# Causal attention on one core: score banks seeded with minus the row maximum by ScalarE, maxima turned in 32x32 blocks and spread by DMA

## The reference

```python
latent_kv = x @ w_kv_down                # 256 -> 128
kv = latent_kv @ w_kv_up                 # keys and values of 16 heads of 64
q = x @ w_q
att = einsum('bqhd,bkhd->bhqk', q, k) * 64 ** -0.5
att = where(causal, att, -inf)
att = softmax(att, axis=-1)              # exp(att - max of the row) / sum
y = einsum('bhqk,bkhd->bqhd', att, v)
return y @ w_out
```

## Time and profile before

| | before |
|---|---|
| median of the runs | 2116.74 us |
| lowest and highest | 2111.61, 2118.76 us |
| span of the profiled execution | 2113.7 us |
| TensorE busy | 94% |
| VectorE busy | 63% |
| ScalarE busy | 52% |
| GpSimd busy | 67% |
| attention's exponentials, first and last start | 292.2 and 2014.6 us |

### The profile page before, as it was taken

How to read it: one execution, slowest core, us unless ns; L and a number is a source line. 1 busy time by engine, 2 the same in 40 slices (tenths; PEclk the granted TensorE clock), 3 DMA queues, 4 the chain that set the end, 5 groups by cost and what they waited for, 6 DMA issues and landing times.

```text
span 2113.7 us, 35206 instructions
## 1 busy us (share of the span) xinstructions
PE 1984.7 (94%) x12886; PEld 1240.9 (59%) x12886; DVE 1337.2 (63%) x2728; ACT 1097.9 (52%) x2236; POOL 1425.9 (67%) x812
## 2 busy tenths in 40 slices
PE   8997788999999999999989999999999999999898
PEld 6775454555655555555555655555555555555466
DVE  7786555576656666666665657576756575656443
ACT  5775543455545454545455444545445445444585
POOL 1333225778687878787857687868786878687822
PEclk9998899999999999999999999999999999999999
DMA  3000000000000000000000000000000000000001
GB/s 124 1 1 1 0 7 13 13 19 10 13 18 16 13 19 12 19 10 19 13 12 17 12 20 11 17 12 20 11 18 11 20 11 18 11 14 11 26 26 60
DMA packets 29243, 37.01 MB, mean 18 GB/s; under 512 B 6928, under 2 KB 20368, under 8 KB 29072
## 3 DMA queue, kind: packets, MB, share of 16 engines
q1 hardware_dynamic: 29072, 34.76, 5.4%
HBM read 30.02 MB, written 4.46 MB: 16 GB/s over the span
## 4 chain that ended last, share of the span: by engine, by line
PE 63%; DVE 14%; POOL 12%; ACT 6%; issue 4%; DMA 1%; POOLq 0%; ACTq 0%; SPq 0%; DVEq 0%
PE heads_out L918 16%; POOL acc L1416 10%; PE beside L723 9%; PE scores L723 7%; PE two_heads L874 7%; PE scores L897 4%; PE scores L903 4%; PE scores L899 4%; PE scores L901 4%; DVE part_max L1112 3%; ACT prob L1331 2%; PE two_heads L723 2%; PE beside L929 2%; PE heads_out L723 1%; DVE wQK_lo L1073 1%
## 5 line engine op out<-in xcount | busy, mean ns | idle before, releaser
L1416 POOL TENSOR_TENSOR acc<-acc,prob 128x1024 f32<-128x1024 f32 (+3 forms) x512 | 1017.9, 1988 | 195.4 <-ACT prob L1331 140.1
L1331 ACT ACTIVATE prob<-scores 128x512 f32<-128x512 f32 (+3 forms) x1280 | 579.4, 539 | 649.2 <-PE scores L903 289.0
L1112 DVE TENSOR_REDUCE part_max<-two_heads 128x2 f32<-128x1024 f32 x384 | 469.3, 1222 | 280.5 <-PE two_heads L874 279.7
L918 PE MATMUL heads_out<-prob,V 128*64 128x512 f32 (+3 forms) x2560 | 544.4, 547 | 0.0
L1109 DVE CUSTOM_DVE_ANT_0 two_heads<-two_heads,mask 128x128 f32<-128x128 f32 (+3 forms) x512 | 242.0, 514 | 180.4 <-PE two_heads L874 180.4
L874 PE MATMUL two_heads<-k_hi,q_hi 64*128 64x512 f32 (+3 forms) x1280 | 274.1, 424 | 62.8 <-DVE part_max L1112 30.6
L918 PEld LDWEIGHTS heads_out<-prob,V 128*64 128x64 f32 x2560 | 156.7, 137 | 232.4 <-issue 209.6
L874 PEld LDWEIGHTS two_heads<-k_hi,q_hi 64*128 64x128 f32 x1280 | 120.6, 184 | 256.6 <-issue 133.4
L897 PE MATMUL scores<-q_hi,k_hi 64*128 64x512 f32 (+3 forms) x1280 | 236.1, 364 | 0.8 <-DVE k_lo L1100 0.5
L903 PE MATMUL scores<-neg_max,sel 64*128 64x512 f32 (+3 forms) x1280 | 235.6, 362 | 0.0
L901 PE MATMUL scores<-q_lo,k_hi 64*128 64x512 f32 (+3 forms) x1280 | 235.5, 362 | 0.0
(11 more groups left out here) (301 smaller groups left out, 2898.7 us busy)
## 6 DMA issues: line engine op xcount, KB each, us to landing
rden<-rden_rows SPq DMA_DIRECT2D x128, 128.0 KB, 2.9
X<-u SPq DMA_DIRECT2D x8, 512.0 KB, 8.7
out<-X SPq DMA_DIRECT2D x8, 512.0 KB, 2.9
wQK_raw<-wQuery SPq DMA_DIRECT2D x16, 192.0 KB, 3.1
wO_raw<-wOut SPq DMA_DIRECT2D x16, 128.0 KB, 2.8
wV_raw<-wValue SPq DMA_DIRECT2D x8, 128.0 KB, 2.9
den<-den_rows SPq DMA_DIRECT2D x64, 4.0 KB
rden_rows<-den SPq DMA_DIRECT2D x64, 4.0 KB, 1.3
```

The lines of the kernel that those rows point to most:

```text
L918: made = pe.matmul(heads_out[head(h), x0:], V[vn % NVS][:, tt, p % 2, head(h)], prob[step % NPROB][:, h, x0:], start=t == 0, stop=t == TPB ...
L1112: made = ve.reduce_max(part_max[:, t, :, c:c + 1], two_heads[:, :, 0:width], AX.X)
L1331: ac.activation(prob[step % NPROB][:, h, x0:], bank(task, h)[:, x0:], ACT.Exp).then_inc(empty(task, h)[0], 1)
L1416: po.tensor_tensor(total[:, :, x0:], total[:, :, x0:], new[:, :, x0:], ALU.add).then_inc(acc_ok, 1)
```

## The change

The fourth pair of score matmuls goes, and `sel`, `neg_max` and the task `turn_max` with it.

- A task `seed` for each step stands an iteration ahead of its score: ScalarE writes minus the maxima, from SBUF into the columns of both score banks that the step uses, in one instruction over both heads. It waits until the banks are emptied. The score's three pairs of matmuls then add to what is there (none of them starts anew), once `seeded` has the seed's number. Where a bank of the step was last used by a task that doesn't write the whole of it, TensorE first runs an opening matmul on each bank (`opened`), and the seed waits for that.
- The maxima are needed on all 128 partitions, `top`, two slots (`NMAX` is 2). VectorE's `minus_max` reduces into the 8 first columns of a tile of 32 columns and transposes it in 32x32 blocks; `rows_out`, four DMAs, writes the rows to DRAM (`top_rows`, four slots); three iterations later `spread_max` reads 4 KB back onto each of the 128 partitions. The spread waits for the last seed of two units before.
- ScalarE takes the exponential of both heads in one instruction, which releases both banks; the score signals once for both. The mask in PSUM stays on VectorE.
- The counting of GpSimd's sums is split over two semaphores; `part_max` has its heads ahead of its tiles; `den` and some tiles lie elsewhere in SBUF; a value or project task starts its bank once, not once for each half.

```diff
@@ planner
+        elif kind == "seed":
+            _, idx, t = task
+            n = 2 * (self.step_of[idx, t] % 2)
+            self.seed_free[idx, t] = sorted({self.freed[b] for b in (n, n + 1) if self.freed[b]})
+            if not (self.whole[n] and self.whole[n + 1]):
+                self.opened[idx, t] = len(self.opened) + 1
+            self.seeds[idx, t] = len(self.seeds) + 1, list(self.count)
...
             idx = self.next_maximum()
             if idx is not None:
-                fillers.append((s + 2, self.start[idx] - 4, ("turn_max", idx)))
+                spreads.append((s + 2, "rows_out", idx))
...
             while self.at < goal - 1:
                 maximum()
+            if self.layers_done:
+                for step in steps[s + 2:s + 4]:
+                    self.need("seed", *step)
+            for at, kind, idx in spreads[:]:
+                if at <= s and (kind == "rows_out" or self.unseeded(idx - NMAX)):
+                    spreads.remove((at, kind, idx))
+                    self.need(kind, idx)
+                    if kind == "rows_out":
+                        spreads.append((s + 6, "spread_max", idx))
             for idx, t in steps[max(0, s - 2):s]:
                 self.need("weigh", idx, t)
@@ tensor_program
-                elif kind == "turn_max":
...
-                    for t in range(TPB):
-                        made = pe.transpose(bank(task)[:, t * P:(t + 1) * P], row_max[:, t, :, :].rearrange("p a b -> p (a b)"), ident[:, :])
-                    made.then_inc(full(task)[0], 1)
+                elif kind == "seed" and task[1:] in plan.opened:
...
+                    first = 2 * (step_of[idx, t] % 2)
+                    for h in range(2):
+                        made = pe.matmul(scores[:, first + h, :], axT_hi[:, 0, 0:P], axT_hi[:, 0, 0:BLK], start=True, stop=True)
+                    made.then_inc(opened, 1)
                 elif kind == "score":
...
-                    for h in range(2):
-                        pe.matmul(bank(task, h)[:, x0:], sel[head(h), :], neg_max[idx % NMAX][head(h), x0:], start=False, stop=True).then_inc(full(task, h)[0], 1)
+                    w.wait_ge(seeded, plan.seeds[idx, t][0])
...
+                    for n, (k, q) in enumerate(terms((k_hi[g], k_lo[g]), (q_hi[i], q_lo[i]))):
+                        for h in range(2):
+                            made = pe.matmul(scores[:, first + h, x0:], k[head(h), kc], q[head(h), x0:], start=False, stop=n == 2, skip_group_check=True)
+                    made.then_inc(full(task)[0], 1)
@@ vector_program
-                    ve.reduce_max(row_max[:, :, :, 0:1], part_max[:, :, :, 0:j + 1], AX.X).then_inc(row_max_ok, 1)
+                    ve.reduce_max(row_max[:, 0:2 * TPB].rearrange("p (h t) -> p h t", h=2), part_max[:, :, :, 0:j + 1], AX.X).then_inc(row_max_ok, 1)
+                    w.wait_ge(row_max_ok, idx + 1)
+                    ve.transpose(rows[:, idx % 2, :], row_max[:, :]).then_inc(rows_ok, 1)
@@ scalar_program
-                    ac.activation(neg_max[idx % NMAX][:, :], bank(task), ACT.Copy, scale=-1.0).then_inc(empty(task)[0], 1)
+                elif kind == "seed":
+                    _, idx, t = task
+                    x0 = P * max(0, t - TPB * UNITS[idx][2])
+                    first = 2 * (step_of[idx, t] % 2)
+                    w.wait_ge(*top_here(idx))
+                    if task[1:] in plan.opened:
+                        w.wait_ge(opened, plan.opened[idx, t])
+                    else:
+                        for b, n in plan.seed_free[idx, t]:
+                            w.wait_ge(emptied[b], n)
+                    ac.activation(scores[:, first:first + 2, x0:], top[idx % NMAX][:, :, x0:], ACT.Copy, scale=-1.0).then_inc(seeded, 1)
...
-                    for h in range(2):
-                        w.wait_ge(*full(task, h))
-                        ac.activation(prob[step % NPROB][:, h, x0:], bank(task, h)[:, x0:], ACT.Exp).then_inc(empty(task, h)[0], 1)
+                    ac.activation(prob[step % NPROB][:, :, x0:], scores[:, first:first + 2, x0:], ACT.Exp).then_inc(empty(task)[0], 1)
@@ sync_program
+                elif kind == "rows_out":
+                    idx = task[1]
+                    w.wait_ge(rows_ok, idx + 1)
+                    if idx >= NTOP:
+                        w.wait_ge(*top_here(idx - NTOP))
+                    for n in range(0, P, SQ):
+                        sp.dma_start(top_rows[idx % NTOP, :].rearrange("(a x) -> a x", x=P)[:, n:n + SQ],
+                                     rows[n:n + 2 * TPB, idx % 2, :]).then_inc(top_out[idx % 2], 16)
+                elif kind == "spread_max":
+                    idx = task[1]
+                    w.wait_ge(top_out[idx % 2], 64 * (idx // 2 + 1))
+                    if idx >= NMAX:
+                        w.wait_ge(seeded, plan.seeds[last_step(idx - NMAX)][0])
+                    sp.dma_start(top[idx % NMAX].rearrange("p h x -> p (h x)"), top_rows[idx % NTOP:idx % NTOP + 1, :].broadcast_to([P, 2 * BLK])).then_inc(top_in[idx % 2], 16)
```

More of the change, by code:

```diff
@@ L41 @@
          (8, "updated"): ["maximum"], (8, "mixed"): ["maximum", ("key", 1), ("query", 1), "maximum"],
-         (8, "tail"): [("turn_max", 0), ("latent", 0, 2), ("value", 0, 0)], (8, "products"): ["maximum", ("value", 0, 1)], (8, "end"): ["maximum"],
+         (8, "tail"): [("rows_out", 0), ("latent", 0, 2), ("value", 0, 0)], (8, "products"): ["maximum", ("spread_max", 0), ("value", 0, 1)], (8, "end"): ["maximum"],
          (9, "updated"): ["maximum"], (9, "mixed"): ["maximum", ("turn_tiles", 0, 12), "maximum"],
          (9, "products"): ["maximum"], (9, "end"): ["maximum", ("turn_tiles", 0, 14), "pair"], (10, "updated"): ["maximum", "pair"]}
+WHOLE = ("query", "key", "latent", "value", "project", "score")
 WAITING = {("ssm_front", 0): 48, ("turn", "a", 0): 14}
@@ L82, in __init__ @@
         self.side_bank = 7
-        self.kinds, self.nth, self.masked = {}, {}, {}
+        self.kinds, self.nth = {}, {}
+        self.whole, self.seeds, self.seed_free, self.opened, self.masked = [False] * 8, {}, {}, {}, {}
         self.start, self.step_of, self.at = [], {}, 0
@@ L95, in take @@
         for g in groups:
+            for b in g:
+                self.whole[b] = task[0] in WHOLE
             free = [self.freed[b] for b in g if self.freed[b]]
@@ L138, in add @@
             self.roots[task] = self.n_roots
-        elif kind in ("query", "key", "value", "turn_max", "latent", "denominators", "turn_tiles", "project"):
+        elif kind in ("query", "key", "value", "latent", "denominators", "turn_tiles", "project"):
             self.take(task, self.one_bank())
@@ L453, in early @@
         def early(task):
-            return self.layers_done or task[0] in ("turn_tiles", "latent") or task[1] < {"key": 2, "query": 2, "turn_max": 2, "value": 1}.get(task[0], 0)
+            return self.layers_done or task[0] in ("turn_tiles", "latent") or task[1] < {"key": 2, "query": 2, "value": 1}.get(task[0], 0)
         for s in range(0, len(steps) + 2, 2):
@@ L712, in attention_memory @@
         def attention_memory(w):
-            for kind in ("query", "key", "turn_max"):
+            for kind in ("query", "key"):
                 w.wait_ge(*full((kind, NU - 1)))
@@ L722, in product @@
                 for n, (l, r) in enumerate(pairs):
-                    made = pe.matmul(dst, l, r, start=first and n == 0, stop=last and n == len(pairs) - 1)
+                    made = pe.matmul(dst, l, r, start=first and n == 0, stop=last and n == len(pairs) - 1, skip_group_check=not first)
                 return made
@@ L939, in tensor_program @@
                         cs = slice((2 * half + q) * P, (2 * half + q + 1) * P)
-                        made = product(bank(task)[:, q * C:(q + 1) * C], terms((oT_hi[:, cs], oT_lo[:, cs]), (wO_hi[n % 2][:, :], wO_lo[n % 2][:, :])))
+                        made = product(bank(task)[:, q * C:(q + 1) * C], terms((oT_hi[:, cs], oT_lo[:, cs]), (wO_hi[n % 2][:, :], wO_lo[n % 2][:, :])), first=q == 0)
                     made.then_inc(full(task)[0], 1)
@@ L1117, in vector_program @@
                     if x0 >= 0:
-                        first = plan.bank[task][0][0][0]
+                        first = 2 * (step_of[idx, t] % 2)
                         w.wait_ge(att_const, 2)
-                        for h in range(2):
-                            w.wait_ge(*full(task, h))
+                        w.wait_ge(*full(task))
                         ve.tensor_tensor(scores[:, first:first + 2, x0:x0 + P], scores[:, first:first + 2, x0:x0 + P],
@@ L1320, in scalar_program @@
                     x0 = P * max(0, t - TPB * UNITS[idx][2])
+                    first = 2 * (step % 2)
                     if not step:
@@ L1404, in gpsimd_program @@
                     total, new = acc[idx % 2], prob[step % NPROB]
-                    for h in range(2):
-                        w.wait_ge(*empty(("score", idx, t), h))
```

(1 more changed line is left out.)

136 lines of the change are left out of this document (67 added, 69 removed).

## The result

| | before | after |
|---|---|---|
| median of the runs | 2115.32 us | 2308.86 us |
| lowest and highest | 2111.61, 2118.76 us | 2303.09, 2313.0 us |
| ratio, 95% interval | | 1.091 (1.0884 to 1.0936) |
| span of the profiled execution | 2113.7 us | 2301.8 us |
| mean granted clock | 0.980 | 0.947 |

The account below looks back on a forecast made before the run. TensorE, busy 94% of the span, was taken as the bound, with GpSimd second. The terms summed to 2113.7 - 115 + 30 + 20 + 5 = 2053.7 us of span; the forecast was 2050 us, range 1970 to 2120.

Parts of the forecast that it names:

- TensorE's relief: Score matmuls and transposes of maxima removed from TensorE: 160 us if always the bound, 115 us taken by the chain's share.
- a term for it: VectorE's second maximum of an iteration comes sooner after the first: 0.06 us for each of 320 iterations, 20 us added.
- The seeds' busy time is hidden.: ScalarE: about 83 us a group with seeds, below TensorE's 96 to 99, so the seeds' busy time costs nothing.
- The wait for bank 0: Seeds wait for VectorE to take a filler's rest from score bank 0: 50 x 0.6 = 30 us, bounds 0 and 100.
- Maxima run up to 20 steps ahead: DMA and SyncE: maxima complete some 20 steps ahead, so the spread costs nothing; 48 us if late.
- The clock: Rival (d), attention: granted clock 0.98, not the expected 1.00, costs 34 us, about 2090; 4 in 100.
- GpSimd as the next bound: GpSimd's 37.5 us meets TensorE's about 37 in the 41.8 us unit; nothing added beyond the chain's share.
- rival (b): GpSimd's sums and loss at unit changes hold the pace, 1 to 2 us a group won: 2085 to 2100; 16 in 100.
- (c): Rival: seeds too late every iteration, behind filler copies in ScalarE's queue; slower from 0.50 us wait, 2180; 14 in 100.
- signs of being wrong: Seeds over 1.1 us, score waits over 0.5 us in most iterations, attention clock under 0.98, or spread after first seed due.
- just in time: Replay of one full iteration: seeds end at 4.9 and 5.9 us, TensorE's next scores stand at 4.8 to 6.1.
- Rival (e): TensorE not relieved because banks must be opened at each step, or gains and waits cancel: 2110 to 2123; 6 in 100.

Follow-up runs that it names:

- b4: The kernel before without the fourth pair of score matmuls, nothing in its place, exponential's input scaled by zero: 2056.3 us, ratio 0.9734.
- e10: The changed kernel with the spread one iteration after the rows, seeds of 64 columns a head and the exponential's input scaled by zero: 2075.2 us.
- b1: The kernel before with an iteration's second filler in the side bank, not in score bank 0: 2261.6 us, ratio 1.0701.
- e6: The changed kernel with the spread one iteration after the rows, not three, and the second filler in the side bank, not score bank 0: 2255.8 us.
- e1: The changed kernel with the spread of the maxima one iteration after the rows are written, not three: 2211.5 us, ratio 1.0458.

## Why the prediction was wrong, point by point

- **TensorE's relief, 115 us with the pair's 89 to 125 in it.** Wrong: the pair is worth 57 us (b4). The turned maxima, 35 us of the 160, were never taken out by themselves. The step that failed is "line 903 stands in the whole chain with 89 us": a chain is followed back along the last releaser, and work that ended shortly before it isn't on it. In b4 it is the reduction of the maxima that moves up: the weight loads' wait for it goes from 72.3 to 137.5 us. How closely behind it had ended before was not measured. I had a term for it, 20 us with bounds 0 and 50; it belongs to the pair's removal, and by b4 it is at most 68.
- **The seed's duration, 1.03 us.** Right: 1026 ns.
- **"The seeds' busy time is hidden."** The worst step. I compared ScalarE's 83 us a group with TensorE's 96 and called the difference cover. In e10 a cut of 397 us of seeds gave 136 us, so 0.34 of each microsecond was paid where I had put none. "Without that cover each 0.1 us of seed would cost 64 us" was the sentence to keep: 0.62 us less a seed gave 136 us, that is 22 us for each 0.1. Busy sums hide nothing if the work stands in a ring of two bank pairs. Whether the 136 us come from the time that the banks are taken or from the place in ScalarE's queue stays open.
- **The wait for bank 0, 50 x 0.6 = 30 us, bounds 0 and 100.** Of the right kind and too small. I priced a seed behind a filler; the square b1, e6 shows the other side of it, that bank 0 was worth 147 us and is worth 44 in e1, 47 in the changed kernel. Seeds waited 105.0 us for project sums alone, which I had mentioned with "some project tiles like them" and not counted. The project filler's tie to GpSimd's `oT_lo` was in the code and in no term.
- **"Maxima run up to 20 steps ahead", spread at nothing, 48 us if late.** Wrong in its premise. The lead of 20 steps is that of a single maximum over the score step of the same number. A unit's last maximum is only about 22 less its own length ahead of its first score: 10 steps for a unit of 12. The rows go out 2 steps later, the spread 6 after that, and the seeds stand 2 ahead of the score: nothing is left. I checked the slots of the unit after a four-step one, and not this count. But the count alone doesn't make the stop: the 16-step unit's spread stands in the list just ahead of its first seeds too, and no seed of a 16-step unit waited for `top`, since SyncE went from its rows straight to its spread. The 12-step unit has both, no lead and two units' denominators' DMAs between its rows and its spread. I had named this queue ("SyncE also carries the `den` round trip") and priced it at 48 us if late; it cost 97 us, 16 stops of 5.5 us and what follows each.
- **The clock, 4 in 100 at 0.98.** It came to 0.93 to 0.98 in the stretches of 100 us from 400 to 2100. The waits were not spread but came as stops of some 5 us, with 0.60 in the six microseconds after one; in e1, without them, the mean of the whole kernel is 0.967, 0.947 with them.
- **GpSimd as the next bound.** Its chain share doubled, as rival (b) had it, and its busy share fell, from 67% to 62%. Shares of a chain that goes round in a circle name a member of the circle. Removing 778 us of its work gave 59 us.
- **The rivals.** (c), with 14 in 100, had the sign and a part of the place: seeds late in ScalarE's queue, decisive from 0.50 us an iteration, 2180. The seeds were of 1.03 us, not 1.28, and still it was 2309; TensorE's matmuls waited for seeds 130 / 320 = 0.4 us an iteration and its weight loads 217 / 320 = 0.7 us, which may partly be the same time; to this came GpSimd's 182 us more for `oT_hi`. Half of the loss, the 97 us of the late spread, was in no rival. It was among the signs of being wrong, as a spread that lands after its first seed is due, and so was a granted clock under 0.98 in attention; both came. What misled me was the replay of one iteration that fits "just in time": seeds that end at 4.9 and 5.9 us for scores that stand at 4.8 to 5.4 and 5.5 to 6.1 leave no room for any delay. Rival (e)'s first half can be ruled out: banks were opened in four steps, not in each.

## What to carry to other kernels

Work moved to an idle engine is free only if the resource that it holds meanwhile (here a pair of PSUM banks, and a place in an in-order queue) was idle too; cost it by how long the ring through that resource gets, not by busy sums. Before a saving on the bounding engine is counted, look for the engine that ends shortly behind it, and where it can be done, measure the saving with nothing put in its place: b4 would have shown 57 us where I had 89 to 125. Where a value must be complete before it is sent, count the lead from its last part, in steps of the planner, subtract every delay written into it, and look at what stands ahead of the transfer in its queue.

## What the runs showed of the hardware

ScalarE copies 128x1024 float32 from SBUF to PSUM in 1026 ns and 128x128 in 280 ns, and takes the exponential of 1024 columns from PSUM in 1022 ns, but these two differ in function too. At 512 columns the changed kernel has three copies: 608 ns from SBUF to PSUM, 621 from SBUF to SBUF (`oT_hi`, written as fp32r), 585 from PSUM to SBUF. The forecast drew on the Trainium skill, ScalarE: Activation LUTs, section "Step-by-step: what each stage is for", for a faster path into PSUM; from SBUF the copy into PSUM is 13 ns shorter here, 2%, with another output type. A spread of one row of 4 KB to 128 partitions (512 KB) landed in 4.0 us (median of 64), and after a stop of 5.3 us TensorE came back with a pair of matmuls each 0.42 us where the earlier trace rows has 0.23, at a granted clock of 0.60 over six microseconds. VectorE's 32x32 turn of a 128x32 tile took 211 ns.
